# Two-layer model on one core: another place for the attended halves and their turns, and reciprocal roots taken by VectorE

## What is computed

```python
q, k = elu(q) + 1, elu(k) + 1
kv = einsum('bnhd,bnhm->bhdm', k, v)
z = 1 / (einsum('bnhd,bhd->bnh', q, k.sum(1)) + 1e-6)
out = einsum('bnhd,bhdm,bnh->bnhm', q, kv, z)        # then out @ w_out.T + b_out
```

```python
def _lresnet(x, y, w):
    z = x + w * y
    inner = -z[..., :1] ** 2 + sum(z[..., 1:] ** 2, -1, keepdims=True)
    return sqrt(C) * z / sqrt(clip(-inner, EPS))
```

## Time and profile before

| what | us |
|---|---|
| median of 3 runs | 2031.93 (2031.28 to 2034.19) |
| the profiled execution | 2035.27 |
| span of its instructions | 2033.5 |
| busy in the span: TensorE | 1402.9 |
| VectorE | 1363.0 |
| ScalarE | 1219.8 |
| GpSimd | 1213.2 |

### The profile page before, as it was taken

One profiled execution on the slowest core, in us unless ns is written; L12 is line 12 of the kernel. 1 busy time (PEld: TensorE's weight loads), 2 busy tenths in 40 slices (PEclk: granted clock), 3 DMA queues, 4 the chain that ended last, 5 costly groups with the idle time before them and its releaser, 6 DMA issues. The chain is left out here.

```text
span 2033.5 us, 63622 instructions
## 1 busy us (share of the span) xinstructions
PE 1402.9 (69%) x21833; PEld 995.6 (49%) x21834; DVE 1363.0 (67%) x3576; ACT 1219.8 (60%) x3356; POOL 1213.2 (60%) x1312
## 2 busy tenths in 40 slices
PE   3479999655555555544233428999999779999947
PEld 3335555544444444432122315666666556666636
DVE  7878887633333333332666649999999568888848
ACT  8548888533333333322556657888886457777746
POOL 6668887211111111114888638999997567777747
PEclk9999999877777777777567769999999989999959
DMA  8547778534344444445566635666665412222228
GB/s 254 170 137 209 209 208 200 114 91 93 91 93 93 93 93 93 93 109 169 155 204 192 186 103 109 123 133 124 126 127 112 84 40 52 52 53 53 54 69 280
DMA packets 495355, 256.26 MB, mean 126 GB/s; under 512 B 359357, under 2 KB 484864, under 8 KB 494720
## 3 DMA queue, kind: packets, MB, share of 16 engines
q1 hardware_dynamic: 482658, 219.11, 44.2%
q0 software_dynamic: 12576, 35.67, 5.5%
HBM read 79.52 MB, written 73.44 MB: 75 GB/s over the span
## 5 line engine op out<-in xcount | busy, mean ns | idle before, releaser
L1513 POOL TENSOR_TENSOR all_late<-experts_se,all_mhalf 128x4 f32<-128x4 f32 (+1 forms) x77 | 76.3, 991 | 465.9 <-DVE experts_se L1703 460.2
L241 PE MATMUL ps<-all_late,l_xq_T 128*128 128x352 f16 x1536 | 252.6, 316 | 61.1 <-DMA l_xq_T<-l_apart 34.6
L241 PE MATMUL ps<-moe_E,experts_hT 128*128 x432 | 92.9, 342 | 251.2 <-DMA experts_hT<-experts_hs 251.0
L241 PEld LDWEIGHTS ps<-all_late,l_xq_T 128*128 (+1 forms) x1536 | 146.9, 99 | 153.1 <-DVE ffn_h L739 45.8
L241 PE MATMUL ps<-l0moe_W,all_xT_all 128*128 128x16 f16 (+2 forms) x1152 | 189.5, 311 | 30.1 <-ACT all_xT_all L940 22.3
L1636 ACT ACTIVATE all_late<-ps 128x510 f32<-128x510 f32 x72 | 42.6, 592 | 277.2 <-PE ps L1564 273.7
L1708 DVE TENSOR_SCALAR experts_se<-experts_so 128x2 f32<-128x2 f32 x72 | 12.2, 169 | 268.5 <-ACT l0moe_W L1638 268.5
L241 PEld LDWEIGHTS ps<-moe_E,experts_hT 128*128 128x128 f16 x432 | 47.0, 117 | 273.6 <-issue 261.8
L241 PE MATMUL ps<-l_Wq,all_xT_all 128*128 128x256 f16 x384 | 75.2, 356 | 151.8 <-DVE both_y L1973 145.6
L2339 POOL TENSOR_TENSOR all_late<-ret_pm,all_late 128x512 f16<-128x512 f32 x128 | 145.4, 1157 | 19.4 <-ACT all_late L2245 19.4
L241 PEld LDWEIGHTS ps<-l0moe_W,all_xT_all 128*128 128x128 f16 x1152 | 83.7, 100 | 112.3 <-ACT all_xT_all L940 26.0
(11 more groups left out here) (300 smaller groups left out, 4643.5 us busy)
## 6 DMA issues: line engine op xcount, KB each, us to landing
rows_dram<-all_late SPq DMA_DIRECT2D x72, 256.0 KB
ret_v<-ret_vpad SPq DMA_DIRECT2D x256, 64.0 KB, 2.0
front_xin<-x SPq DMA_DIRECT2D x16, 512.0 KB, 4.6
x_dram<-front_x SPq DMA_DIRECT2D x16, 512.0 KB, 5.4
all_late<-x_dram SPq DMA_DIRECT2D x64, 128.0 KB
z_dram<-all_late SPq DMA_DIRECT2D x64, 128.0 KB
both_zin<-z_dram SPq DMA_DIRECT2D x16, 512.0 KB, 4.3
both_xin<-x SPq DMA_DIRECT2D x16, 512.0 KB, 4.6
```

What stands on the lines that cost most here:

```text
L241: mm = pe.matmul(out, lhs[a], rhs[b], start=first and n == 0, stop=last and n == 2, skip_group_check=True)
L1513: pool.tensor_tensor(rows[:, n % 4, which, :, 0], se[:, u, which], power[:, which], ALU.pow).then_inc(s_time, 1)
```

## The change

In the experts' phase, SyncE's table issues `turn_attended` with a lag of 14 steps in place of 10, and GpSimd's step has `attended_lo` ahead of `times`, with a lag of 6 in place of 8. In the combining phase GpSimd's `pow` is gone, and VectorE takes the roots between `inner` and the second half of `result`: the bits of x are shifted right by one as an integer, subtracted from a constant, and three Newton steps of three instructions each follow. These are 11 instructions on [128, 3, 4], each waiting for the one before; the last raises the semaphore that `pow` raised.

```diff
 # phase_experts, SyncE
-            unrolled(count, [(7, turn_hidden), (0, turn_rows), (11, store), (10, turn_attended)])
+            unrolled(count, [(7, turn_hidden), (0, turn_rows), (11, store), (14, turn_attended)])
 # phase_experts, GpSimd
             for n in range(count + OLAG):
+                if n % 2 == 0 and 0 <= n - 6 < TILES:
+                    attended_lo((n - 6) // 2)
                 times(n)
-                if n % 2 == 0 and 0 <= n - 8 < TILES:
-                    attended_lo((n - 8) // 2)
 # phase_combine, GpSimd
-                pool.tensor_tensor(norm[:, u, which], diff[:, u, which], power[:, which], ALU.pow).then_inc(s_norm, 1)
...
-                if live(i):
-                    roots(i)
 # phase_combine, VectorE
+            def roots(i):
+                u, which = i % LAG, live(i)
+                x, y, squared, rest = (v[:, u, which] for v in (diff, norm, sq, part))
...
+                root_step(dve.tensor_scalar(seed[:, u, which], x.bitcast(I32), 1, None, ALU.arith_shift_right))
+                root_step(dve.tensor_scalar(y.bitcast(I32), seed[:, u, which], -1.0, RSQRT_SEED, ALU.mult, ALU.add))
+                for n in range(3):
+                    root_step(dve.tensor_tensor(squared, y, y, ALU.mult))
+                    root_step(dve.scalar_tensor_tensor(rest, squared, -0.5, x, ALU.mult, ALU.mult))
+                    last = dve.scalar_tensor_tensor(y, rest, 1.5, y, ALU.add, ALU.mult)
+                    if n < 2:
+                        root_step(last)
+                last.then_inc(s_norm, 1)
...
                 if group(i - 2) or group(i - 3):
                     inner(i)
+                if live(i):
+                    roots(i)
                 if group(i - 4):
                     result(group(i - 4), 1)
```

More of the change, by code:

```diff
@@ L59 @@
 PAD_ROWS = 8
+RSQRT_SEED = float(0x5f3759df)
 EXPERT_LAG = 6
@@ L1752, in phase_combine @@
         grow, weight = ph.sb("grow", [P, LAG, G]), ph.sb("weight", [P, LAG, G])
-        power = ph.sb("power", [P, 3, G])
+        seed = ph.sb("seed", [P, LAG, 3, G], I32)
+        sq, part = small("sq"), small("part")
         s_x, s_zin = (ph.slot_sems(n) for n in ("xload", "zload"))
@@ L1757, in phase_combine @@
         s_ss = [None] + [ph.sem(f"ss{k}") for k in (1, 2)]
-        s_fill, s_grow, s_growth, s_first, s_sqr, s_diff, s_max, s_norm = ph.sems("fill grow growth first sqr diff max norm")
+        s_root, s_grow, s_growth, s_first, s_sqr, s_diff, s_max, s_norm = ph.sems("root grow growth first sqr diff max norm")
         s_weight, s_ob, s_y1, s_y2, s_y3, s_gate, s_sg, s_x1 = ph.sems("weight ob y1 y2 y3 gate sg x1")
@@ L1995, in inner, with root_step @@
                 dve.tensor_scalar(diff[:, u, which], diff[:, u, which], EPS_T, None, ALU.max).then_inc(s_max, 1)
+            rooted = [0]
+            def root_step(ins):
+                rooted[0] += 1
+                ins.then_inc(s_root, 1)
+                dve.wait_ge(s_root, rooted[0])
+            def roots(i):
+                u, which = i % LAG, live(i)
+                x, y, squared, rest = (v[:, u, which] for v in (diff, norm, sq, part))
+                if group(i - 1):
+                    dve.wait_ge(s_first, i)
+                if i > 1:
+                    dve.wait_ge(s_max, i - 1)
+                if group(i - 5):
+                    dve.wait_ge(s_gate, i - 4)
+                root_step(dve.tensor_scalar(seed[:, u, which], x.bitcast(I32), 1, None, ALU.arith_shift_right))
[7 more added lines that the diff above has]
+                last.then_inc(s_norm, 1)
             weights.dve_begin(dve)
```

2 lines of the change are left out of this document (removed).

## The result

| what | before | after |
|---|---|---|
| median, us | 2032.26 (4 runs, 2031.28 to 2034.19) | 1747.64 (4 runs, 1745.32 to 1750.54) |
| profiled execution, us | 2035.27 | 1745.32 |
| its span, us | 2033.5 | 1743.5 |

The ratio of the times is 0.8599 (0.8584 to 0.8615): 284.6 us less by the medians, 290.0 by the spans of the two profiled executions. 1735 was forecast, 12.6 us too low, inside the range of 1705 to 1800. The 290.0 us divide so: GpSimd's last root of the experts' phase starts at 675.8 in place of 942.0 (266.2 us), the combining phase takes 22 us less, what follows 1.8 us.

A forecast was written before the change was run, and what follows sets the result against it. SyncE's queue waiting for GpSimd's low half bounded the experts' phase, GpSimd bounded combining. From 2035.3 us, -279 (experts) and -18 (combining) gave 1738, or 1735 against the median of 2031.93; range 1705 to 1800.

The forecast's parts named there:

- one stop: Experts' phase: SyncE's 305.3 us wait for the low half and TensorE's 251.0 us for turned hidden values share one cause.
- the low clock: Rival, experts' phase: TensorE stays at 1.2 GHz, 12.8 us a pair, 149 us more, 1884 us; chance 3%.
- serial transfers: Rival, experts' phase: SyncE's transfers run one behind the other, 20.3 us a pair, 2123 us; chance 2%.
- no effect: Rival, experts' phase: TensorE's stop has another cause, the turn costs nothing, only -18 or 0 is left; chance 1%.
- 8.0 forecast: Experts' phase: a pair of steps falls from 16.78 to 8.0 us, most of the -279 us forecast there.
- the root still has a good part of a step: Experts' phase: the wait on `attended_hi`, moved ahead of `times`, leaves GpSimd's root enough time, the earlier turn having landed.
- My loop of 13.5 us in four steps: Experts' phase: turn, landing, high and low half, root, splits, SyncE's issues; 6.7 us a pair, not the bound.
- The upper bound of 9.4 a pair: Experts' phase: nearly full resources queue up, 43 us more, 1778 us; lock or queueing together had 17%.
- a new wait: Rival, experts' phase: such as `attended_hi` waiting for a late turn; 10 to 13 us a pair, 1797 to 1890; chance 7%.
- the lower bound of 7.3: Experts' phase: SyncE's six issues fill 7.2 us a pair, 7.3 with the gap to the next.
- The lock between VectorE and GpSimd: Rival, experts' phase: SBUF instructions of both engines exclude each other, 9.6 us a pair, 1785; lock or queueing 17%.
- -18 forecast: Combining phase: roots on VectorE cut rounds from 13.6 to 12.0 us, less a dearer tail; bounds -23 and +2 us.

The follow-up runs named there:

- e6: The kernel after with the lag of `turn_attended` at 12 in place of 14; 1726.80 us, ratio to the kernel before 0.8475 to 0.8504.
- e4: The kernel after with the lag of `turn_attended` back at 10, so only the low half's edit in the experts' phase; 1749.60 us.
- e11: The kernel after with the lag of `turn_attended` at 12 and `attended_lo`, still lag 6, behind `times`; 1746.43 us, ratio to before 0.8563 to 0.8595.
- e5: The kernel after with `attended_lo`, still lag 6, behind `times`, the turn's lag kept at 14; 1733.51 us, ratio to before 0.8511 to 0.8541.
- e1: The kernel before with the experts' phase edits alone, combining's roots still on GpSimd; 1768.83 us, ratio to before 0.8674 to 0.8716.
- e9: The kernel after with two Newton steps in place of three for combining's roots; 1739.92 us, ratio to before 0.8543 to 0.8579.
- e2: The kernel after with the experts' edits undone, so only combining's roots on VectorE; 2034.85 us, ratio to before 0.9983 to 1.0014.
- c2: Repeat, in another group of runs, of combining's edits alone against the kernel before; 2041.22 us, ratio to before 1.0009 to 1.0028.
- c1: The kernel after, unchanged, run a third time as a control; 1777.43 us, ratio to before 0.8710 to 0.8739.

## Why the prediction came out as it did

**The stop and its removal: right.** SyncE's wait and TensorE's for `experts_hT` were one stop. It went whole, with TensorE's granted clock at 0.98, where it had been 0.69; the rivals of the low clock, of serial transfers and of no effect fell. The 184 GB/s are the "about 180 GB/s and more" of the forecast.

**The pair of steps: 8.0 forecast, 8.37 measured.** This term is about as large as the whole miss of 12.6 us: 31 x 0.37 = 11. That the rest cancelled is luck: combining gave 4 us more than forecast and the phases behind it 1.8, while the profiled execution, which lay 3.3 us above the median before, lay 2.3 below it after. The step that failed is the sentence that "the root still has a good part of a step" behind `attended_hi`, with the cover named there, "that the turn of the pair before the last ... has landed". It had not: 27 of 32 times ScalarE waited for it, 36.5 us. My loop of 13.5 us in four steps left out that the lag of 14 makes the turn wait its place in SyncE's list, though all is ready: from the end of the low half to the turn I had a root of 1.01, two splits of 0.41 and some 6 us of issues, 7.8 in all, and it was 11.0. The loop was 16.7 us, and e6, e4 and e11, where it is open, have shorter pairs. The upper bound of 9.4 a pair came without a working of its own. It was in the rivals as a new wait, at 10 to 13 us a pair; the wait came, but cost 0.5 to 0.8 us a pair. e6 (7.75) and e11 (7.59) show what the pair is without it, between the lower bound of 7.3 and the 8.0. The lag of 14 and the low half ahead of the root each cost little without the other: 7.87 (e5) and 7.75 (e6) against 7.59 with neither (e11, on another chip).

**The lock between VectorE and GpSimd, 9.4 to 9.6 a pair: wrong in size, not in kind.** It is shown below.

**Combining: -18 forecast, -22 measured in the first runs and on B; about nothing on A (-2 to +3 us), 4 to 7 us more on C.** The reference throughout is the 236.9 us of the first run; e1's 237.1 on A agrees with it. The working held by its parts: 0.205 us a link for my 0.22, rounds of 12.0 us for my 12.0, the bound gone from GpSimd to VectorE (e9), the gathers of a group at 10.9 us for my 11.3 ((756.03 - 690.88) / 6 in GpSimd's timeline), the tail dearer (10.0 us a round where it was 8.4). On A too the rounds outside the stretch are as fast: four rounds, between the starts of `result` at 1016.03 and 1063.51 in e2, take 47.5 us, as in the kernel after (735.91 to 783.35), and 54.3 in the kernel before (1009.31 to 1063.65). What no step of the working held is the stretch: that for 15 to 30 us VectorE's and ScalarE's instructions can start later, in one group of runs and not in another. On A (e2) the medians of the two kernels differ by 1.4 us, on C (c2) the kernel with the new roots is 0.1 to 0.3% slower.

**The sum.** The median of 1747.64 and the ratio stand on the runs in which the stretch did not occur; with it the same change gives 0.8710 to 0.8739, 1777 us, still inside the range.

## What to carry to other kernels

When a queue stops at a transfer, find the smallest move that makes it ready in time: moving both the transfer and its producer turned a stop of 7.6 us a pair into a new one of 0.6, and only runs of each edit alone showed it. Read the length of the phase in the trace beside the median, since a gain of 15 to 19 us in one phase was hidden by a loss of 20 to 25 in another. Repeat the control on the chip of each group before explaining a difference of 1%.

## What the runs showed of the hardware

**The same small dependent instructions of VectorE can cost three to seven times as much in another group of runs, on another chip.** In the groups on A and C, but not in that on B, links of 0.20 us took 0.70 or 1.40 within 15 to 30 us near the start of combining, and again in short stretches on C. In e1, on A, with GpSimd's roots, no such stretch was found. But e1 differs in two ways: VectorE has no chain of 11, and GpSimd's gathers are broken by a root of 2.31 us each round. Which of the two the stretch needs was not tried. In c1 the slow links end at 740.2, some 4 us after GpSimd's row of gathers pauses; whether the gathers, the supply of instructions or something else holds the links was not tried, and stays open, as do ScalarE's waits of 9 us at L543.

**VectorE and GpSimd do hold each other up, but only where GpSimd's work is large.** In the kernel before `hidden_lo` never took over 0.43 us, though roots of [128, 4] ran beside it. Where it meets the low half of [128, 512] it is otherwise. GpSimd's and VectorE's timelines of e6:

```profile
541.06 1.16 POOL L1500 TENSOR_TENSOR experts_o<-l0moe_kv_sum,experts_o 128x512 f16<-128x512 f32 x1 [1.81 <-ACT experts_o L1620]
542.18 1.19 POOL L1514 TENSOR_TENSOR all_late<-experts_se,all_mhalf 128x4 f32<-128x4 f32 x1
```
```profile
541.50 1.00 DVE L1723 TENSOR_TENSOR experts_hs<-all_late,experts_hs 128x256 f16<-128x256 f32 x1
```

`hidden_lo` takes 1.00 us and ends at 542.50, 0.28 us after the low half, and the root behind it takes 1.19 in place of 1.01. In e6 this happens to 29 of the 72 `hidden_lo` (over 0.5 us, 1.26 at most): whatever their start, all 29 end 0.28 us after the low half's end. In the kernel after it happens to 5; there 4 low halves, which started with a `hidden_lo` or up to 0.2 us behind it, are stretched to as much as 1.44; in e11, where the order is the other one, to none: 0.425 us at most. The Trainium skill, "SBUF — State Buffer", section "SBUF: two separate sides", speaks of a lock for the whole instruction between such a pair; for the low half the trace agrees nearly (a `hidden_lo` of 0.42 us that ends 0.28 after it has begun 0.14 before its recorded end, as an estimate), for the small root it does not. The price in e6 was 15.3 us of VectorE's time in the whole phase (what those 29 took beyond 0.42 each), 0.5 us a pair, on an engine that was busy for 201.54 of the 235 us from 400 to 635, far from the 1.6 us a pair of the rival. It is no part of the 8.37 us: the kernel after lost 3.5 us to it in all.
